# Scatter-adding node sums into three copies in place of four, in a graph network layer on one core

## What is computed

```python
h = jnp.maximum(_layernorm(x, axis=-1), 0.0)
h = jnp.concatenate([h[col], edge_attr], axis=1)      # 206250 x 128, col = dst
h = jax.nn.relu(h @ W1.T + b1)
h = jax.nn.relu(h @ W2.T + b2)
summed = jax.ops.segment_sum(h, row, num_segments=n)  # row = src
cnt = jax.ops.segment_sum(jnp.ones(...), row, num_segments=n)
agg = summed / jnp.maximum(cnt, 1.0)[:, None]
z = jax.nn.relu(jnp.concatenate([h_nodes, agg, u[batch]], axis=1) @ Wa.T + ba)
x = x + z @ Wb.T + bb
```

## Time and profile before

| | |
|---|---|
| median of 3 runs | 1965.5 us (1960.17 to 1968.19) |
| the profiled execution | 1965.07 us |
| its span in the profile | 1963.3 us |
| granted TensorE clock, mean | 0.954 of full speed |
| start, up to the first scatter | 97 us |
| loop, 940 scatters | 97 to 1897 us |
| end | 1897 to 1963 us |

### The profile page before, as it was taken

The page is one execution under the profiler, slowest core; times in us unless marked ns, Lnnn a source line. Parts: engine busy times, 40 slices in busy tenths (PEclk is TensorE's granted clock), DMA queues, the critical chain, the costliest instruction groups (busy, mean ns, idle before and its releaser), DMA issues.

```text
span 1963.3 us, 42045 instructions
## 1 busy us (share of the span) xinstructions
PE 1728.9 (88%) x12463; PEld 1473.0 (75%) x12463; DVE 1383.5 (70%) x3570; ACT 1116.8 (57%) x2531; POOL 1536.2 (78%) x983
## 2 busy tenths in 40 slices
PE   3498888899999999999999999999999999977817
PEld 2376777688888787888878888887888888866715
DVE  7876566677677777777767777777777777744528
ACT  3275666566666665666656666666566666632203
POOL 6078888888888888888888888888888888887850
PEclk9699899999999999999999999999999999988959
DMA  7598888899999999999999999999999999997756
GB/s 268 198 197 154 140 154 150 170 193 199 182 197 205 195 196 197 192 205 188 193 195 194 191 204 192 197 198 206 199 188 203 198 200 204 202 213 148 155 125 197
DMA packets 321982, 372.08 MB, mean 190 GB/s; under 512 B 42432, under 2 KB 203552, under 8 KB 321248
## 3 DMA queue, kind: packets, MB, share of 16 engines
q1 hardware_dynamic: 185280, 306.11, 54.4%
q0 software_dynamic: 135360, 62.15, 33.7%
q10 hardware_dynamic: 1120, 1.11, 0.2%
HBM read 203.93 MB, written 159.27 MB: 185 GB/s over the span
## 4 chain that ended last, share of the span: by engine, by line
POOL 46%; PE 21%; issue 16%; DMA 10%; DVE 6%; ACT 1%; SPq 0%; POOLq 0%; ACTq 0%; DVEq 0%
POOL sums L797 40%; DMA sums<-regA,idx 8%; PE bank L1228 5%; POOL sums L785 5%; PE bank L1276 5%; PE bank L1250 4%; PE bank L1239 3%; PE bank L1266 2%; ACT regA L894 1%; DVE regC L1127 1%; DVE regC L986 1%; DVE regC L992 1%; DVE regC L1081 1%; DMA src<-rows_src 1%; DMA regC<-in_src_cols 1%
## 5 line engine op out<-in xcount | busy, mean ns | idle before, releaser
L797 POOL DMA_INDIRECT sums<-regA,idx x844 | 1354.7, 1605 | 324.0 <-issue 242.9
L1228 PEld LDWEIGHTS bank<-h,regC 128*128 128x128 f32 x3072 | 393.9, 196 | 209.7 <-ACT h L906 174.2
L1228 PE MATMUL bank<-h,regC 128*128 128x130 f32 x3072 | 427.9, 283 | 89.5 <-ACT h L906 89.1
L1276 PE MATMUL bank<-w,h 128*128 128x128 f32 x3224 | 435.3, 279 | 0.0
L1250 PE MATMUL bank<-regA,L 128*128 128x512 f32 x806 | 422.5, 606 | 2.9 <-DVE regA L1046 2.4
L1276 PEld LDWEIGHTS bank<-w,h 128*128 128x128 f32 x3224 | 402.5, 196 | 1.0 <-ACT h L886 0.6
L894 ACT ACTIVATE regA<-bank 128x520 f32<-128x520 f32 x211 | 127.3, 603 | 409.4 <-DMA sums<-regA,idx 351.1
L886 ACT ACTIVATE h<-bank 128x512 f32<-128x512 f32 x403 | 238.6, 592 | 156.1 <-PE bank L1250 144.2
L1239 PE MATMUL bank<-regC 128*128 128x129 f32 x2352 | 300.0, 281 | 15.7 <-ACT vscat L917 9.2
L1266 PEld LDWEIGHTS bank<-h,regC 128*128 128x128 f32 x1688 | 222.6, 192 | 118.2 <-issue 95.8
L906 ACT ACTIVATE h<-bank 128x512 f32<-128x512 f32 x403 | 239.8, 595 | 122.4 <-PE bank L1276 119.1
(11 more groups left out here) (142 smaller groups left out, 1279.3 us busy)
## 6 DMA issues: line engine op xcount, KB each, us to landing
regC<-slots SPq DMA_DIRECT2D x294, 260.0 KB, 5.0
regA<-in_ea SPq DMA_DIRECT2D x202, 256.0 KB
slots<-regC SPq DMA_DIRECT2D x192, 260.0 KB
src<-rows_src SPq DMA_DIRECT2D x107, 256.0 KB
slots<-regC SPq DMA_DIRECT2D x192, 138.1 KB
sums<-regA,idx POOLq DMA_INDIRECT x844
dstR<-rows_dst SPq DMA_DIRECT2D x101, 128.0 KB
sums<-zeros SPq DMA_DIRECT2D x20, 645.0 KB, 7.3
```

The lines of the kernel that those rows point to most:

```text
L797: nc.gpsimd.indirect_dma_start(out=sums[k], out_offset=bass.IndirectOffsetOnAxis(ap=idx[:, n % RING, t:t + 1], axis=0), in_=scat[:, n % 4, ...
L1228: last = T.matmul(psSlot(t)[:, k, :], place, h2[:, g % 2, t, :], start=True, stop=True)
L1276: last = T.matmul(psL2(g % 2)[:, t * H:(t + 1) * H], h1[:, g % 2, t * TILE:(t + 1) * TILE], w2[:, :], start=False, stop=True, skip_group_c ...
```

## The change

`NSETS` goes from 4 to 3, so that the scatters take three copies in turn. The copies hold the same sum between them. With it change:

- the zeroing: 15 DMAs in place of 20 (the five of the last copy are gone, with the last three entries of `ZAFTER`);
- the landing that a scatter waits for: that of the third scatter before it in place of the fourth;
- the end: 39 loads in place of 52; the first of VectorE's two sums over the copies is half as wide, and the second adds the third copy to its result;
- the limit of the general path's flag is one lower (59 rows without a place in place of 60).

```diff
-NSETS = 4
+NSETS = 3
-ZAFTER = (0, 1, 1, 1, 1, 1, 2, 2)
+ZAFTER = (0, 1, 1, 1, 1)
...
-        s1 = take(2 * KC).rearrange("p (k c) -> p k c", k=2)
+        s1 = take(KC)
...
-            VE.memset(midc[:, 2:3], -float(TPG * PLACES + OVER))
+            VE.memset(midc[:, 2:3], -float(TPG * PLACES + OVER - 1))
...
-                    link(VE.tensor_tensor(s1[:, :, 0:m * C], SA[:, s, 0:2, 0:m * C], SA[:, s, 2:4, 0:m * C], ALU.add))
-                    link(VE.tensor_tensor(s2[:, 0:m * C], s1[:, 0, 0:m * C], s1[:, 1, 0:m * C], ALU.add))
+                    link(VE.tensor_tensor(s1[:, 0:m * C], SA[:, s, 0, 0:m * C], SA[:, s, 1, 0:m * C], ALU.add))
+                    link(VE.tensor_tensor(s2[:, 0:m * C], s1[:, 0:m * C], SA[:, s, 2, 0:m * C], ALU.add))
```

## The result

| | before | after |
|---|---|---|
| median | 1964.9 us (4 runs, 1960.17 to 1968.19) | 2156.7 us (4 runs, 2144.7 to 2159.36) |
| ratio | | 1.096, 95% interval 1.093 to 1.099 |
| the profiled execution | 1965.1 us | 2159.1 us |
| its span | 1963.3 us | 2157.4 us |
| first scatter to last | 96.7 to 1895.5, 1798.7 us | 96.7 to 2098.5, 2001.8 us |

The change costs 192 us. The loop is 203.1 us longer and the end 9.0 us shorter: 194.1 us, the difference of the two spans.

What follows compares the result with a forecast made beforehand. GpSimd, going from one scatter straight to the next, was taken to bound the kernel. From the profiled 1965.1 us, +164 for waits, -2 at the start and -6 at the end gave 2121, so 2120 us; range 2015 to 2190.

Steps and rivals of the forecast that it cites:

- What bounds the kernel: In the loop, GpSimd goes straight from scatter to scatter: 940 starts by 1.91 us; anything put between lengthens the kernel.
- The wait: Before each loop scatter: the third-back landing must be in, at three turns, 5.55 us at least; 59 of 166 readings later.
- Its price: In the loop, 937 scatters by a mean lateness of 0.175 us: +164 us.
- the third correction: In the loop, other traffic thins out and fewer scatters queue, so each landing comes 0.2 us sooner.
- correction (1): In the loop, a wait moves later starts too, so the two scatters behind wait less: less than 223 us.
- correction (2): In the loop, GpSimd may restart slower than ScalarE after a landing, 0.1 to 0.2 us per wait: 285 us.
- The start: At the first scatters, the fourth's 5.40 us wait for zeroes goes, but later groups come no sooner: -2 us.
- The end: After 1897 us, VectorE's smaller first sum saves 6.4 us and fewer loads 0.4 us: together -6 us.
- A: The forecast itself: third-back waits in a quarter to a third of scatters, landings slightly sooner; 2050 to 2180 us, chance 0.72.
- B: Rival for the loop: landings get no sooner, or later in a convoy of three; 2180 to 2240 us, chance 0.10.
- C: Rival for the loop: with fewer under way, landings come 0.6 to 1.0 us sooner; 1990 to 2040 us, chance 0.12.
- D: Rival for the loop: nearly every landing within three turns' 5.55 us, only savings left; 1957 us, chance 0.06.

## Why the prediction was right, and where it was off

The forecast was slower, 2120 us between 2015 and 2190; it is 2156.7.

**What bounds the kernel.** Right. A pause that put 0.04 us between two scatters lengthened the kernel by nearly as much for each, less DMA traffic with four copies shortened it by 7 us only, and TensorE took 68 us longer in a loop whose growth the waits of GpSimd account for.

**The wait.** Right in mechanism. 251 to 269 waits (more than 250 were forecast) and 297 us of them after the change (about 240 were forecast), and the wait put on four arrays alone gives the same time as three arrays. Of the readings before it, two are inexact: three turns of 1.54 + 0.30 us are 5.52 us (the starts lie 1.85 apart, which gives the 5.55), and landings were waited for 21 times before the change, not 18.

**Its price.** Too low: +164 us forecast. The waits on landings beyond issue are 216.5 us after, and 5.2 us before; less the 5.1 us that the start gives, that is near the loop's +203 us. The term at fault is the third correction, 0.2 us off every landing. The mean landing did come sooner, by 0.17 us, which is what was taken. But a wait comes only from a landing longer than three turns, and the longest tenth came 0.1 us sooner. With 0.1 us off in place of 0.2, the same 166 readings give 937 x 0.205 = 192 us, and 1965 + 192 - 8 = 2149 against 2157. Left out altogether, 0.24 x 937 = 223 us, the correction would have cost less as well: 2180, 23 us off in place of 37.

**What was luck in it.** Whether corrections (1) and (2) cancel can be reckoned from the trace of before, as an estimate. Take for each scatter its last recorded update as its landing, and let it start when the one before has ended and the idle time of the trace has passed (0.30 us where that held a wait on a landing), and not before the third one back has landed and GpSimd's 0.27 us have passed too. Replayed so, the loop grows by 218 us; with every landing 0.1 or 0.2 us sooner by 198 or 178 us, and 203 were measured. The rule with the fourth one back gives the old loop to 0.1 us. So the 223 us that the prediction set out from were near 218, but not for its reasons. ScalarE starts 0.10 us after a landing's last update; with that added, the mean lateness over 937 scatters is 0.28 us (262 us in all) and not the 0.24 of the 166 readings, which are only of places where ScalarE waited. With GpSimd's 0.27 us it is 0.35 us, 329 us in all, so correction (2) is +67 us; and the replay takes 111 us off for correction (1). A sample that was 39 us too low and a correction (1) that was 44 us larger than correction (2) made up for each other by luck. The readings of ScalarE can mislead further: in the kernel after, 142 of them have a mean of 5.61 us, though the mean landing there is shorter than before.

**The start.** -2 us forecast, up to -5; a kernel with only this wait removed gained 3.1 us (0.1% to 0.4% by its interval).

**The end.** -6 us forecast, up to -8. By a kernel of its own -6.8 us; in the spans 9.0 us, of which 1.6 lie behind the last chunk's first sum and come in a kernel with the old end too. The rest, 7.3 us, is 0.5 us ahead of the first chunk, where 0.4 was forecast, and 6.9 between the chunks, where VectorE's 12 x 0.53 = 6.4 were.

**The rivals.** The time lies in A's range. B (nothing sooner) is nearer than C, as the long landings nearly kept their length. D, by which all landings fit into three turns, fails: even with most of two kinds of loads left out, at a DMA share of 0.73 between 300 and 1500 us, three copies waited 134 us. The rule of the Trainium skill beside it, about 2 us and the bytes by the bandwidth ("DMA: Bandwidth & Descriptors", section "Anatomy of one DMA — SWDGE (gpsimd) path"), makes a landing 3.7 us after the scatter's start, an estimate that is near the fastest tenth here (under 3.3 to 3.6 us, of which 1.54 are GpSimd's own) and far from the others. That the queues were quiet in those cases, as the prediction had it, no row shows. The same page says in "Latency and other measured facts" that lighter HBM load makes a smaller fixed cost; the traces agree in direction: ScalarE's readings went from 5.29 to 4.76 us when the loads were thinned.

## What to carry to other kernels

When a ring of buffers or copies is made shorter, don't compare its length with the mean latency: put each latency beside the distance of the turn that must cover it, and average only what sticks out. Here the mean landing, 5.3 us, lay under the 5.7 us of three turns, and the loop still lost 11%. If landings are expected to get shorter, ask which: here the mean came 0.17 us sooner and the slowest tenth, which stuck out, 0.1 us. And ask whether the cases that can be read stand for all: here those that ScalarE showed were late by 0.24 us in the mean, and all of them by 0.28.

An experiment that adds a wait should replace one, not stand beside one. The second wait before each scatter cost 84 us of its own, which could have been taken for the price of the landings.

## What the runs showed that I had not expected

- Two waits ahead of a scatter instead of one: GpSimd starts 0.73 us after a landing at the soonest, with one 0.27 us; 2248.0 against 2163.8 us for the same order of work. Why was not settled.
- GpSimd's elementwise sums beside VectorE's in the end: for each full sum of GpSimd (1491 ns in the mean) one of VectorE's large operations took 1.33 to 1.81 us in place of 0.70. Dividing the work between the two lost 5.7 us.
- A memset of 0.73 us on GpSimd that follows a scatter is nearly free: it overlaps the scatter's last part, and the distance of two starts grew by 0.04 us.
